# A transformer layer on eight cores: the output projection of row tiles 4 to 15 interleaved with the first feed-forward product of row group 0

## What is computed

```
x: (4, 4096, 1024) float32
a  = layernorm(x)
q, k, v = a Wq, a Wk, a Wv               16 heads of 64
s  = (q k^T - slope_h |i - j|) / 8, causal;  ctx = softmax(s) v
x2 = x + layernorm(ctx Wo + bo)
h  = quantize_256(layernorm(x2) w1 + b1)            4096 columns
h  = piecewise-linear Gelu(h), 32 equal pieces of 1/4 on [-4, 4], quantized to 1/256
out = x2 + layernorm(quantize_256(h w2 + b2))
```

## Time and profile before

| | us |
|---|---|
| median of 3 executions | 1283.11 |
| lowest, highest | 1282.63, 1376.25 |
| the profiled execution | 1280.45 |
| its span, slowest core (first to last instruction) | 1278.9 |
| spans of the eight cores | 1274.8 to 1278.9 |

### The profile page before, as it was taken

One profiled execution on the slowest core, in us unless ns is written; L12 is line 12 of the kernel. 1 busy time (PEld: TensorE's weight loads), 2 busy tenths in 40 slices (PEclk: granted clock), 3 DMA queues, 4 the chain that ended last, 5 costly groups with the idle time before them and its releaser, 6 DMA issues.

```text
span 1278.9 us, 27226 instructions; the slowest of 8 cores (1274.8 to 1278.9 us)
## 1 busy us (share of the span) xinstructions
PE 1159.5 (91%) x11195; PEld 644.4 (50%) x11328; DVE 762.7 (60%) x1694; ACT 1009.7 (79%) x1293; POOL 152.9 (12%) x341
## 2 busy tenths in 40 slices
PE   3999989999999999999987995668999999999996
...
DVE  7967343433434243343421895998888888888842
ACT  3579999999999999999997786888777777777710
...
GB/s 260 273 140 51 90 73 59 68 67 52 83 57 69 68 35 52 26 27 35 23 96 184 229 221 177 97 90 83 108 109 107 111 111 108 124 124 107 75 67 66
DMA packets 62727, 127.89 MB, mean 100 GB/s; under 512 B 9478, under 2 KB 26118, under 8 KB 61964
## 3 DMA queue, kind: packets, MB, share of 16 engines
...
...
HBM read 117.73 MB, written 25.17 MB: 112 GB/s over the span
## 4 chain that ended last, share of the span: by engine, by line
PE 72%; ACT 14%; DVE 7%; DMA 4%; issue 2%; POOL 0%; SPq 0%; DVEq 0%; POOLq 0%; ACTq 0%
PE pO L869 17%; PE pF L797 13%; PE pjb L312 10%; PE pjb L344 8%; PE S L406 8%; ACT P L421 8%; PE acc L450 8%; PE pW L658 3%; DVE kst L322 2%; DMA xst<-x_full 2%; PE pja L312 1%; ACT cu L812 1%; ACT g L830 1%; ACT g L827 1%; ACT hq L855 1%
## 5 line engine op out<-in xcount | busy, mean ns | idle before, releaser
L421 ACT ACTIVATE P<-S,biasT 128x1024 bf16<-128x1024 f32 (+3 forms) x640 | 572.7, 1010 | 29.2 <-PE S L406 28.1
L797 PE MATMUL pF<-xl2T,w1s 128*128 128x512 bf16 x1004 | 257.2, 382 | 30.9 <-ACT cu L812 26.1
L869 PE MATMUL pO<-w2s,hq 128*128 128x512 bf16 x1002 | 250.4, 379 | 1.2
L406 PE MATMUL S<-Q,K 64*128 64x512 bf16 (+3 forms) x1280 | 181.9, 351 | 16.0 <-ACT P L421 13.6
L450 PEld LDWEIGHTS acc<-V,P 128*128 128x128 bf16 x4352 | 166.3, 97 | 55.4 <-DVE ctx L469 12.3
L450 PE MATMUL acc<-V,P 128*128 128x66 bf16 x4352 | 185.4, 193 | 3.0 <-DVE ctx L469 2.5
L797 PEld LDWEIGHTS pF<-xl2T,w1s 128*128 128x128 bf16 x1024 | 98.4, 98 | 159.4 <-ACT cu L812 40.1
L312 PE MATMUL pjb<-xlT,W 128*128 128x512 bf16 x573 | 155.0, 381 | 17.8 <-issue 6.3
L869 PEld LDWEIGHTS pO<-w2s,hq 128*128 128x128 bf16 x1024 | 100.2, 98 | 120.8
L322 DVE CAST kst<-pjb 128x512 bf16<-128x512 f32 x81 | 56.0, 691 | 143.1 <-PE pjb L312 138.6
L827 ACT ACTIVATE g<-cs 128x512 f32<-128x512 int32 x128 | 80.5, 629 | 69.3 <-DVE cs L819 69.2
...
## 6 DMA issues: line engine op xcount, KB each, us to landing
w1s<-w1bf SPq DMA_DIRECT2D x128, 256.0 KB, 2.7
...
K<-kst SPq DMA_DIRECT2D x128, 64.0 KB, 2.1
Q<-kst SPq DMA_DIRECT2D x128, 64.0 KB, 2.1
w1bf<-w POOLq DMA_DIRECT2D x32, 256.0 KB, 4.6
w2s<-w POOLq DMA_DIRECT2D x8, 1024.0 KB, 31.2
...
```

The lines of the kernel that those rows point to most:

```text
L406: t = put("tensor", lambda io, o=o, r0=r0: io.matmul(S[s][:, o * 512 + c0:(o + 1) * 512], K2[pb][hh][r0:r0 + 64, j * 128:(j + 1) * 128], Q ...
L421: t = put("scalar", lambda io: io.activation(out=P3[:, :, c0:512], in_=S[s][:].rearrange("p (o c) -> p o c", o=2)[:, :, c0:512], func=AF.E ...
L797: t = put("tensor", lambda io, c=c: io.matmul(pF[b][:], w1s[n % 4][:, c * 128:(c + 1) * 128], xl2T4[:, NG - 1 - g, c, :], start=(c == 0), ...
L869: put("tensor", lambda io, ft=ft, hf=hf: io.matmul(pO[b][:, hf * 512:(hf + 1) * 512], slot_of(g, ft, tl), w2s[:, ft * 1024 + hf * 512:ft * ...
```

## The change

It has five parts.
1. The first 7 steps of the output projection (n = 0 to 6) run alone; the 12 that follow are cut into 62 pieces by the generator `c_parts` and issued between group 0's 32 ticks, two after nearly every tick.
2. PSUM: pW has two buffers instead of three; pF has two buffers during group 0 and four from group 1 on (the added two lie where pU lay); the second product's pO is pW.
3. SBUF: hq lies over ctx, x2 has four buffers in the last 16 KB of w2s, into which x is loaded directly, and from the end of the projections on. The last two of the eight loads of w2 (`w2b`) are issued after the last x2 tile is done with, and only the second product's blocks from 24 on wait for them.
4. `c_xm` is gone: x2 is kept as x + rs pW, without the term nm of the first layer norm, which is kept in `nmx` (the layer norm over x2 does not see a constant per row). `o_b` adds nmx to its own nm in one more POOL operation.
5. `f_g` is issued two ticks behind instead of one, and f_d, f_y, f_m and f_hq one tick later with it.

```diff
-        pW = [ps(st_c, f"pW{i}", 1024, F32) for i in range(3)]
-        pU = [ps(st_c, f"pU{i}", 1024, BF16) for i in range(2)]
+        pW = [ps(st_c, f"pW{i}", 1024, F32) for i in range(2)]
+        pF = [ps(st_c, f"pF{i}", 512, F32) for i in range(2)]
+        st_u = contextlib.ExitStack()
+        pU = [ps(st_u, f"pU{i}", 1024, BF16) for i in range(2)]
+        st_u.close()
+        pF += [ps(st_c, f"pF{i}", 512, F32) for i in range(2, 4)]
         st_c.close()
-        st_f = contextlib.ExitStack()
-        pO = [ps(st_f, f"pO{i}", 1024, F32) for i in range(2)]
-        pF = [ps(st_f, f"pF{i}", 512, F32) for i in range(2)]
-        st_f.close()
+        pO = pW
...
-                for f in range(0, 32, 4):
-                    t_w2 = dma("gpsimd", w2s[:, f * 1024:(f + 4) * 1024].rearrange("p (f d) -> p f d", f=4),
-                               w2_d[f * 128:(f + 4) * 128, :].rearrange("(f p) d -> p f d", p=128),
-                               "w2", [proj_end])
+                for f in range(0, 24, 4):
+                    t_w2 = load_w2(f, "w2", [proj_end])
...
-        pWfree = [t_ctx] * 3
-        ctxTfree, xinfree, xmfree, xl2free = ([t_ctx, t_ctx] for _ in range(4))
-        x2free = [[t_ctx], [t_ctx]]
+        pWfree = [t_ctx] * 2
+        ctxTfree, xl2free = [t_ctx, t_ctx], [t_ctx, t_ctx]
+        x2free = [[proj_end]] * 4
...
         def c_load(j):
-            C[j, "x"] = dma("sync", xin[j % 2][:], x_d[2 * j * 128:(2 * j + 1) * 128, :], f"xi{j % 2}",
-                            [xinfree[j % 2]])
+            C[j, "x"] = dma("sync", x2[j % 4][:], x_d[2 * j * 128:(2 * j + 1) * 128, :], f"xi{j % 4}",
+                            x2free[j % 4])
...
-            w = j % 3
+            w = j % 2
             k, tk = stats((pW[w][:, 0:512], pW[w][:, 512:1024]), [C[j, "a"]])
             C[j, "k"] = k
-            C[j, "r"] = stats2(k, tk, neg=True)
-
-        def c_xm(j):
-            b, k = j % 2, C[j, "k"]
-            C[j, "xm"] = put("scalar", lambda io: io.activation(
-                out=xm[b][:], in_=xin[b][:], func=AF.Identity, bias=nm[k][:], scale=1.0),
-                after=[C[j, "r"], C[j, "x"], xmfree[b]], inc=True)
-            xinfree[b] = C[j, "xm"]
+            C[j, "r"] = stats2(k, tk)
+            t = put("gpsimd", lambda io: io.tensor_scalar(
+                out=rs[k][:, 2:3], in0=mv[k][:, 0:1], scalar1=-1.0, scalar2=None, op0=ALU.mult), inc=True)
+            C[j, "nm"] = put("gpsimd", lambda io: io.tensor_tensor(
+                out=nmx[:, j:j + 1], in0=rs[k][:, 2:3], in1=rs[k][:, 0:1], op=ALU.mult), after=[t], inc=True)
...
-            b, w, k = j % 2, j % 3, C[j, "k"]
+            b, w, k = j % 4, j % 2, C[j, "k"]
             t = None
             for hf in range(2):
                 sl = slice(hf * 512, (hf + 1) * 512)
                 t = put("vector", lambda io, sl=sl: io.scalar_tensor_tensor(
-                    out=x2[b][:, sl], in0=pW[w][:, sl], scalar=rs[k][:, 0:1], in1=xm[b][:, sl],
-                    op0=ALU.mult, op1=ALU.add), after=[C[j, "xm"], C[j, "r"]] + x2free[b], inc=True)
+                    out=x2[b][:, sl], in0=pW[w][:, sl], scalar=rs[k][:, 0:1], in1=x2[b][:, sl],
+                    op0=ALU.mult, op1=ALU.add), after=[C[j, "x"], C[j, "r"]], inc=True)
             pWfree[w] = t
-            xmfree[b] = t
-            slot_free[k] = [t]
+            slot_free[k] = [t, C[j, "nm"]]
             t_x2s[j] = dma("sync", x2_d[j * 128:(j + 1) * 128, :], x2[b][:], f"xs{b}", [t])
             k2, tk = stats((x2[b][:, 0:512], x2[b][:, 512:1024]), [t])
             C[j, "k2"] = k2
             C[j, "r2"] = stats2(k2, tk, neg=True)
...
+        def c_parts(n):
+
             if n + 1 < NP:
                 c0(n + 1)
+                yield
             if n < NP:
                 c_wo(n)
                 c_sta(n)
+                yield
             if 0 <= n - 3 < NP:
                 c_xt(n - 3)
+                yield
             if 0 <= n - 1 < NP:
-                c_xm(n - 1)
                 c_x2(n - 1)
-                if n + 1 < NP:
-                    c_load(n + 1)
+                yield
             if 0 <= n - 2 < NP:
                 c_xl(n - 2)
+                if n + 2 < NP:
+                    c_load(n + 2)
+                yield
             if 0 <= n - 3 < NP:
                 c_xte(n - 3)
-        t_c1v, t_c1s, t_c1t = ("v", cnt["v"]), ("s", cnt["s"]), ("t", cnt["t"])
+                yield
+
+        for j in range(4):
+            c_load(j)
+        c0(0)
+
+        for n in range(7):
+            for _ in c_parts(n):
+                pass
...
-            a = [F[n, "y"]] + left.get((g, ft // 8), [])
+            a = [F[n, "y"]] + ([C[ft // 2, "left"]] if g == 0 else left[g, ft // 8])
...
-                        after=[t_hq[32 * g + ft], pOfree[b], t_w2] if hf == 0 else ())
+                        after=[t_hq[32 * g + ft], pOfree[b], t_w2 if ft < 24 else t_w2b] if hf == 0 else ())
...
-            F[j, "or"] = stats2(k, tk, neg=True, eps=1e-5 * 65536.0)
+            t = stats2(k, tk, neg=True, eps=1e-5 * 65536.0)
+            F[j, "or"] = put("gpsimd", lambda io: io.tensor_tensor(
+                out=nm[k][:], in0=nm[k][:], in1=nmx[:, j:j + 1], op=ALU.add), after=[t], inc=True)
...
         def chain_step(n, g):
 
             has = lambda i: 0 <= i < len(order)
-            if has(n - 1):
-                f_g(n - 1)
             if has(n - 2):
-                f_d(n - 2)
+                f_g(n - 2)
             if has(n - 3):
-                f_y(n - 3)
-            if has(n - 2):
-                f_m(n - 2)
+                f_d(n - 3)
             if has(n - 4):
-                f_hq(n - 4)
+                f_y(n - 4)
+            if has(n - 3):
+                f_m(n - 3)
+            if has(n - 5):
+                f_hq(n - 5)
             if has(n):
                 f_u(n)
                 f_split(n)
...
-        run(group1(0, range(32)))
+
+        rest = [(n, 6 if 3 <= n < 15 else 5 if n == 15 else 4 if n == 16 else 3 if n == 17 else 2)
+                for n in range(7, NP + 3)]
+        parts = itertools.chain(*(c_parts(n) for n, _ in rest))
+        n_parts, done = sum(k for _, k in rest), 0
+        for ft in range(32):
+            run(group1(0, [ft]))
+            while done < n_parts * (ft + 1) / 32:
+                next(parts, None)
+                done += 1
+        run(parts)
+        t_c1t = C[NP - 1, "xt"][1]
+        t_w2b = None
+        for f in range(24, 32, 4):
+            t_w2b = load_w2(f, "w2b", x2free[0] + x2free[1] + x2free[2] + x2free[3])
+        pFfree += pUfree
+        for b in range(2):
+            x2infree[b], osbfree[b] = C[NP - 1, "a"], C[NP - 1, "a"]
+            otfree[b], pOfree[b] = t_c1t, pWfree[b]
+            x2_load(b)
         for g in range(NG):
             if g + 1 == NG:
                 fin(32 * g + 31)
```

More of the change, by code:

```diff
@@ L125, in build_nc @@
     nm = [sb(f"nm{i}", 1, F32) for i in range(NS)]
+    nmx = sb("nmx", NP, F32)
     zt = [sb(f"zt{i}", 4, F32) for i in range(2)]
     rz = [sb(f"rz{i}", 4, F32) for i in range(2)]
-    R0 = addr["at"]
+    X0 = addr["at"]
+    R0 = X0 + 8 * 1024
     R1 = R0 + 32 * 1024
@@ L154, in build_nc @@
     wos = sb("wos", 8 * 1024, BF16, R2)
[L155 to L167, removed]
+    xl2T = [sb(f"xl2T{g}", 8 * 512, BF16, X0 if g == 0 else R3 + (g - 1) * 8 * K) for g in range(NG)]
+    ctxT = [sb(f"ctxT{i}", 1024, BF16, R3 + (70 + 2 * i) * K) for i in range(2)]
+    xl2 = [sb(f"xl2_{i}", D, BF16, R3 + (74 + 2 * i) * K) for i in range(2)]
+    x2 = [sb(f"x2_{i}", D, F32, R1 + (48 + 4 * i) * K) for i in range(4)]
+    hq = sb("hq", 40 * 512, BF16, X0)
+    x2in = [sb(f"x2in{i}", D, F32, R2 + 4 * i * K) for i in range(2)]
+    osb = [sb(f"osb{i}", D, F32, R2 + (8 + 4 * i) * K) for i in range(2)]
+    ot = [sb(f"ot{i}", D, F32, R3 + (70 + 4 * i) * K) for i in range(2)]
+    w1s = [sb(f"w1s{i}", 1024, BF16, R3 + (62 + 2 * i) * K) for i in range(4)]
+    slots = [R3 + (24 + i * 2) * K for i in range(19)]
     chain = lambda nm_, n, ty: [sb(f"{nm_}{i}", 512, ty, slots.pop(0)) for i in range(n)]
@@ L559, in build_nc, with load_w2 @@
         gen, quota = None, 0.0
+        def load_w2(f, sem, after):
+            return dma("gpsimd", w2s[:, f * 1024:(f + 4) * 1024].rearrange("p (f d) -> p f d", f=4),
+                       w2_d[f * 128:(f + 4) * 128, :].rearrange("(f p) d -> p f d", p=128), sem, after)
         def next_piece(i):
@@ L621, in build_nc @@
         ctx3 = ctx[:].rearrange("p (t c) -> p t c", t=NP)
-        xl2T4 = xl2T[:].rearrange("p (g c n) -> p g c n", g=NG, c=8)
+        xl2T3 = [b[:].rearrange("p (c n) -> p c n", c=8) for b in xl2T]
         pUfree = [t_ctx, t_ctx]
         un = {"i": 0}
-        pWfree = [t_ctx] * 3
-        ctxTfree, xinfree, xmfree, xl2free = ([t_ctx, t_ctx] for _ in range(4))
-        x2free = [[t_ctx], [t_ctx]]
+        pWfree = [t_ctx] * 2
+        ctxTfree, xl2free = [t_ctx, t_ctx], [t_ctx, t_ctx]
+        x2free = [[proj_end]] * 4
```

(30 more changed lines are left out.)

16 lines of the change are left out of this document (7 added, 9 removed).

## The result

The changed kernel takes 1290.24 us (median of 6 executions, 1288.05 at the lowest), the kernel before 1284.34, measured beside it: ratio 1.0054, 95% interval 1.0039 to 1.0069. That is 5.9 us slower by the medians and 6.9 by the ratio, which leaves out the few executions in which the cores of one die showed a lower clock; the forecast was 1273, with a range of 1263 to 1288. The profiled execution took 1288.05 us with a span of 1286.4.

A forecast was written before the change was run, and what follows sets the result against it. DVE, with 143.8 of 183 us, was taken as nearest to a bound in the output projection and group 0, PE in groups 1 to 3. Span 1278.9 - 10.2 + 0.3 = 1269.0, profiled 1270.6, median 2.66 above: 1273 us, range 1263 to 1288.

The forecast's parts named there:

- The ring in the opening: Steps n = 0 to 6: two pW buffers close a loop through DVE's list, 6.97 us a tile, before about 4.8.
- By these rows the opening stays at full clock: Opening: PE idles about 2.2 us in every ring, yet the clock was claimed not to fall to half.
- Rival A: Opening: the clock falls to half, +19.5 us over five rings, 1293 us in all; chance 6 in 100.
- Group 0's start: After the opening: first matmul at 744.9 us, first cs at 749.3, second cs at 755.8, w1 loads behind x2(5)'s store.
- The mixed stage: Group 0 with interleaved projection: DVE binds, 11.7 us a tile, 112.8 us of work from 755.8, ending at 868.6.
- Rival B: Mixed stage doesn't overlap: DVE waits for each tile's product, +22 us, 1295 in all; chance 9 in 100.
- Group 1's first matmul waits for u(30) ... start at 864.5 ... Gain 10.2 us: End of mixed stage: group 1 starts 3.3 us ahead of DVE's s(31) at 867.9, at 864.5 instead of 874.7.
- The second half of w2 ... Nothing to pay: Group 1: the last two w2 loads land at about 879, block 24 needs them at 885; cost 0.
- Rival C: Group 1: w2 lands late, at 892, and PE stands 7 us in tick 6; 1280 us; chance 7 in 100.
- Had the Gelu stayed one tick behind ...: Mixed stage: ACT would wait behind every split; two ticks behind lets it run ahead, without the 0.49 us wait.
- The tail: Last row tile: the added POOL operation, 0.19 us, and a hop of some 0.14 lie on the path: +0.3 us.

The follow-up runs named there:

- experiment 1: Changed kernel with only the 7 opening steps reordered: x2 of tile n-1 with its statistics ahead of tile n's product and first statistics; 1276.34 us, ratio 0.9964.
- experiment 6: Changed kernel with the opening ordered on DVE as x2(n-1), first statistics of n, then statistics of x2(n-1); 1273.56 us, ratio 0.9934.
- experiment 2: Changed kernel with the first four w1 loads issued ahead of the opening instead of behind the load of tile 8; 1278.63 us, ratio 0.9987.
- experiment 3: Changed kernel without the two late w2 loads, blocks 24 to 31 reading w2's blocks 0 to 7 instead; 1284.87 us, ratio 1.0030.
- experiment 5: Changed kernel with w2's last quarter in four 0.5 MB loads, each issued once its x2 buffer has served its last tile; 1284.92 us, ratio 1.0032.
- experiment 4: Changed kernel with the Gelu back at one tick behind its block; 1293.38 us, ratio 1.0101 to the kernel before.
- experiment 8: The kernel before with nothing changed but the Gelu two ticks behind; 1270.17 us, ratio 0.9913.
- experiment 7: Changed kernel with the finer split opening order, the early first w1 loads and the spread w2 loads together; 1258.77 us, ratio 0.9827.
- experiment 10: Experiment 7 without mixing: all 16 row tiles projected ahead of group 0, in the order of experiment 6; 1263.65 us, ratio 0.9865.
- experiment 9: Experiment 7 with the 62 parts spread over 30 ticks instead of 32; 1257.34 us, ratio 0.9818.
- experiment 11: Experiment 7 with the parts spread over 27 ticks instead of 32; 1261.36 us, ratio 0.9853.

## Why the prediction was wrong

The mechanisms it named were nearly all there. Two steps failed: a gain that was the small difference of large terms, taken without the slips that each of them could have, and one cost that was put at nothing.

**The ring in the opening: right.** Forecast 6.97 us a step, measured 7.04. Experiments 1 and 6 show that it was the list's order and not the lost buffer: with two buffers and another order the step is 4.78, what PE needs. The prediction took the ring for the price of two buffers. It cost some 15 us (experiment 6), and the new order brings them back.

**"By these rows the opening stays at full clock": half wrong.** Four of the five later products in the ring ran at full clock, the first, at 708.02, took 5.31 us: +1.7. Rival A came in small, once in the opening. The gap's length alone didn't decide it: after 2.47 us of idle one product ran largely at half clock (708.02) and the next one at full clock (716.68). Half clock came in the mixed stage too, at 847.74 after 3.72 us, and DVE then waited 1.91 us for that product. The Trainium skill, "TensorE: Matmul & The Clock Gate", section "Why this matters for your kernels", warns of long idle gaps between matmul bursts, because the clock then falls to half. The gap of 3.72 us agrees with it; the half clock behind 2.47 us does not follow from it, nor from my reading of the earlier trace rows, which took two gaps for all.

**Group 0's start: right in kind, too early by 6 us.** First matmul 750.9 instead of 744.9: 1.3 us were there before the opening (attention ended later in this execution), 1.7 the half clock, some 1 the first product and the rings together, and 1.9 the w1 load, 4.99 us from issue to landing where the earlier trace rows had shown 3.26 to the matmul. DVE's second cs, where the mixed stage begins, came at 762.31 instead of 755.8: 6.5 late. That the loads stand behind the store of x2(5) was seen; that moving four issues would undo it and bring 8.6 us (experiment 2), was not.

**The mixed stage: right in its bound, 3.6 us short.** 11.67 us a tile against 11.7, DVE full. Rival B didn't come. From 762.3 to 868.0 us DVE was idle for 4.2 us (101.54 busy of 105.7) where the sum had none; its cs(31) came at 878.0 instead of 867.9 (6.5 from the start, 3.6 from here).

**"Group 1's first matmul waits for u(30) ... start at 864.5 ... Gain 10.2 us": the step that failed.** By cs(31) the start would have been 3.3 us ahead of 878.0, at 874.7. It was at 876.4, 1.7 later, because PE's list holds block 31 behind the transposes of tile 15: x2, statistics, POOL, xl and only then PE, 3.80 us idle, and half clock after it. The gain was 10.2 in a stage of 125 us, in which every slip had one sign: 6.5 + 3.6 + 1.7 = 11.8 of the 11.9. The sum had bounded none of the three. So the change won nothing up to here (876.4 against 874.7).

**"The second half of w2 ... Nothing to pay": the other failed step.** I asked when the two loads would land for block 24, and that was right: no matmul waited for w2s. But I did not ask what they do to others. The w1 loads beside them took up to 15.2 us instead of 2.8, and one of them held PE for 2.71 us. Experiments 3 and 5 show that this gap goes with the two loads; the whole kernel gained 3.1 and 2.8 us by them. The rest of the stage's 5.4 us, the slow matmuls, is not shown to be their doing: cores 0 and 1 had them without the loads (experiment 3), the changed kernel had them again at 1012 us, and experiment 6 had the loads without them. Rival C's sign came, a PE gap for a DMA, 15 us into group 1, but for w1 and not w2, and at under half its price of 7 us. The Trainium skill, "DMA: Bandwidth & Descriptors", section "Queues, rings and completion order", says that a DMA engine takes turns between the queues that have work; that w1's loads were late beside the w2 loads fits it, but no run here separates it from other causes.

**"Had the Gelu stayed one tick behind ...": right in sign.** ACT waits in each tick, but it costs only 6 us in the mixed kernel (experiment 4), where DVE is near its bound. The same edit in the kernel before brings 11 us (experiment 8). I had read its wait of 0.49 us as the reason for group 0's slowness, and never worked out what that edit does alone.

**The tail**: +0.3 forecast; the added POOL operation took 0.19 us at 1280.17, as said.

**What it comes to.** By the experiments the change holds two gains, the Gelu's second tick (11 us before, 6 in the mixed stage) and the interleaving (5 us), and three costs that eat them: the ring (15), the late first w1 loads (9) and the w2 loads at the seam (3). With the costs taken out the same idea runs in 1258.8 us, and in 1257.3 with the parts over 30 ticks. These figures don't quite close: experiment 7 is 22 us faster than the kernel before, and the Gelu and the interleaving account for 11 and 5. The other 6 us are what experiment 10 has over experiment 8. So the repairs of experiments 2, 5 and 6 also touch something that the kernel before has too. Its own wait for the first w1 load (3.85 us of PE in front of group 0, core 0) is a candidate, the new order on DVE and the dropped c_xm are others, and no run separates them.

**Left open.** Why four matmuls take 1.05 us in some stretches; what decides between half and full clock after gaps of 2 to 3 us; and how to get the last tiles' chains out from in front of the last blocks: PE's waits for xl(14) and xl(15) together are 5.5 us in experiment 7, 6.3 in 9 and 5.2 in 11. The part of the changed kernel that drops c_xm was not tried alone.
